# Second norm and first relational half: one core, a cut at column 96 of the third layer, scatters moved beside it

## The reference, cut to what matters

```python
h = relu(layernorm(x)); x = x + L0(h, src, dst)
h = relu(layernorm(x)); x = x + L1(h, src, dst, theta)
h = relu(layernorm(x)); x = x + L2(h, ..., src, dst, edge_type_86)
h = relu(layernorm(x)); x = x + L3(h, src, dst)
# L2, for every edge e:
#   msg  = sum_b w_comp[etype, b] * (h[src] @ weight[b])
#   gate = tanh(relu(<h[src] @ A1 + b1, h[dst] @ A2 + b2 + rel[etype]> / sqrt(32)))
#   out  = relu(segment_sum(gate * msg, dst) + h[src of the last edge] @ self_loop_weight)
```

## Time and profile before

| | us |
|---|---|
| median of 3 runs | 2469.23 |
| lowest, highest | 2468.75, 2469.87 |
| the profiled execution's own time | 2470.35 |
| its span in the trace | 2468.6 |

### The profile page before, as it was taken

One profiled execution on the slowest core, in us unless ns is written; L12 is line 12 of the kernel. 1 busy time (PEld: TensorE's weight loads), 2 busy tenths in 40 slices (PEclk: granted clock), 3 DMA queues, 4 the chain that ended last, 5 costly groups with the idle time before them and its releaser, 6 DMA issues.

```text
span 2468.6 us, 12924 instructions
## 1 busy us (share of the span) xinstructions
PE 327.9 (13%) x2316; PEld 243.5 (10%) x2316; DVE 1818.3 (74%) x3200; ACT 388.7 (16%) x1275; POOL 1419.5 (58%) x1426
## 2 busy tenths in 40 slices
PE   0000000201100000010000001066764000034000
PEld 0000000101000000000000001044442000034000
DVE  8998989988699995971889989999999952321000
ACT  0000001010022121200112200177774210000000
POOL 6666776371776047306777720366662177777776
PEclk9999999999999999999999999976666555555555
DMA  1001003000221125100122220000000120100000
GB/s 21 17 9 29 12 16 119 6 12 2 96 66 32 51 67 178 42 34 10 63 71 62 84 77 0 3 8 8 8 8 4 59 69 10 35 12 11 8 8 8
DMA packets 57643, 88.37 MB, mean 36 GB/s; under 512 B 26387, under 2 KB 49864, under 8 KB 56184
## 3 DMA queue, kind: packets, MB, share of 16 engines
q0 software_dynamic: 44864, 19.00, 5.1%
q1 hardware_dynamic: 6872, 43.31, 4.5%
q10 hardware_dynamic: 5856, 25.60, 2.7%
HBM read 37.41 MB, written 54.76 MB: 37 GB/s over the span
## 4 chain that ended last, share of the span: by engine, by line
DVE 59%; POOL 15%; issue 12%; PE 6%; DMA 3%; ACT 2%; DVEq 0%; ACTq 0%; SPq 0%; POOLq 0%
POOL out L1789 9%; DVE mf L589 9%; POOL mf L1783 6%; DVE pay L589 4%; DVE psum L1321 4%; DVE pay L1307 4%; DVE psum L1306 3%; DVE outs L589 3%; DVE z L589 2%; PE psum L2271 2%; DVE z L1602 2%; DVE psum L618 2%; PE psum L2234 1%; DVE mf L1311 1%; DVE xs L1311 1%
## 5 line engine op out<-in xcount | busy, mean ns | idle before, releaser
L1789 POOL DMA_INDIRECT out<-outs,i_src x196 | 200.3, 1022 | 236.9 <-DVE outs L1578 109.2
L1783 POOL DMA_INDIRECT xd<-in_x,i_dst x196 | 205.2, 1047 | 109.7 <-DVE mf L589 55.5
L1783 POOL DMA_INDIRECT xs<-in_x,i_outS x196 | 195.9, 999 | 68.9 <-issue 56.4
L1789 POOL DMA_INDIRECT out<-outs,i_srcX x196 | 199.3, 1017 | 62.3 <-issue 57.6
L589 DVE TENSOR_TENSOR mf<-mf 128x128 f32<-128x128 f32 (+6 forms) x582 | 181.0, 348 | 10.5
L2005 ACT ACTIVATE pay<-pay 128x1248 f32<-128x1248 f32 (+1 forms) x63 | 75.6, 1199 | 647.4 <-DVE pay L1307 627.2
L589 DVE TENSOR_TENSOR pay<-psum,pay 128x512 f32<-128x512 f32 x196 | 130.4, 684 | 16.8 <-ACT pay L2095 14.7
L1602 DVE TENSOR_REDUCE z<-pay 128x512 f32 (+1 forms) x196 | 132.3, 675 | 0.0
L2234 PE MATMUL psum<-pay 128*128 128x512 f16 x196 | 102.7, 524 | 89.3 <-ACT pay L2080 55.6
L1783 POOL DMA_INDIRECT mf<-l_own_rows,lists x50 | 49.8, 996 | 111.9 <-DMA l_own_rows<-xs 97.0
L1783 POOL DMA_INDIRECT mf<-l_own_rows,ptr x46 | 45.9, 998 | 99.1 <-DMA l_own_rows<-pay 85.4
(11 more groups left out here) (521 smaller groups left out, 2726.2 us busy)
## 6 DMA issues: line engine op xcount, KB each, us to landing
outs<-in_x ACTq DMA_DIRECT2D x14, 624.0 KB, 5.4
out<-outs ACTq DMA_DIRECT2D x14, 624.0 KB, 3.0
l_first_rows<-mf SPq DMA_DIRECT2D x2, 3234.0 KB, 9.8
z<-in_x ACTq DMA_DIRECT2D x6, 624.0 KB, 6.0
out<-z ACTq DMA_DIRECT2D x6, 624.0 KB, 2.9
l_own_rows<-pay SPq DMA_DIRECT2D x1, 3430.0 KB, 9.5
payload_by_dst<-z SPq DMA_DIRECT2D x1, 3234.0 KB, 9.5
sums_by_edge<-z SPq DMA_DIRECT2D x1, 3234.0 KB, 17.3
```

The source lines that it names most:

```text
L1783: G.indirect_dma_start(out=dest(k), out_offset=None, in_=table, in_offset=bass.IndirectOffsetOnAxis(ap=idx[:, k:k + 1], axis=0), bounds_ch ...
L1789: G.indirect_dma_start(out=table, out_offset=bass.IndirectOffsetOnAxis(ap=idx[:, k:k + 1], axis=0), in_=source(k), in_offset=None, bounds_ ...
```

## The change

Three parts. (1) The packing into MULTI and FOLLOWING moves from before the dense halves to behind the last part of `first_layer`; one copy is added, which keeps the places (`place_m`), and the memset of `kept` moves behind it. (2) The relational loop is cut behind turn 24 (column 96). Columns 0 to 95 (part A) get their gate, sums, self loop, own rows, norm, fills and first rows at the cut; columns 96 to 195 (B; BH with column 95) get theirs behind the loop. The rows of a partition's first node, whose carry isn't known at the cut, are picked out with masks (`ends`) and written later by two scatters of their own (`heads_out`) and one fill (`head_fill`). (3) POOL sends 38 columns of OUT ahead instead of 12, then one for each tile to the cut, 40 at the pace of DVE's steps in the cut, 22 behind it, then A's 96 fills, one for each tile; 19 of these wait for the last tile.

```diff
-SENDS_AHEAD = 12
+SENDS_AHEAD = 38
+CUT_TURN = 24
+CUT = 4 * CUT_TURN
+HEADC = CUT - 1
+SENDS_BETWEEN = 40
+OWN_BEFORE_HEAD = 36
...
+            for k, (own, part) in enumerate(((XSW, A), (OWNT, B))):
+                sp.wait_ge(s["l3_own_ready"], k + 1)
+                sp.dma_start(own_rows[:, part, :], own[:, part, :]).then_inc(s["l3_own_stored"], 16)
+                sp.wait_ge(s["l3_first_ready"], k + 1)
+                span = slice(part.start * ROWW, part.stop * ROWW)
+                sp.dma_start(first_rows[:, span], first_f[:, span]).then_inc(s["l3_first_stored"], 16)
...
+            ends, free = c["tmp"][:, A], c["tmp2"][:, 0:EC]
+            link(ts(free, col("kn"), FAR / 2, FAR, ALU.is_lt, ALU.mult))
+            link(tt(free, free, col("dst_out"), ALU.add))
+            link(V.tensor_copy(icols["outF"][:, B], free[:, B]))
...
+            for given, out_index in ((free[:, A], head_fill), (c["linear"][:, A], head_row)):
+                link(tt(picked, ends, given, ALU.mult))
+                link(V.tensor_reduce(found_at, picked, AX.X, ALU.add))
+                link(tt(out_index, found_at, none, ALU.add))
+            for k, name in enumerate(("dis", "kn", "dst_out")):
+                link(tt(picked, ends, c[name][:, A], ALU.mult))
+                link(V.tensor_reduce(head_own[:, D + k:D + k + 1], picked, AX.X, ALU.add))
...
+            l2_turns(0, CUT_TURN)
...
+            marks["cut"] = link.n
+            gated(MA, A, 1)
+            running_sums(MA, A)
+            link(V.tensor_copy(cut_sum, Z[:, HEADC, :]))
+            link(tt(Z[:, A, :], Z[:, A, :], CUR[:, A, :], ALU.add))
+            ends = c["tmp"][:, A]
+            link(tt(ends, c["head"][:, A], c["head"][:, 1:CUT + 1], ALU.subtract))
+            for given, out_row in ((Z, head_sum), (XD, head_own[:, 0:D])):
+                link(tt(MA, given[:, A, :], bc(ends), ALU.mult))
+                link(V.tensor_reduce(out_row, MA.rearrange("p c f -> p f c"), AX.X, ALU.add))
+            link(V.scalar_tensor_tensor(out=XD[:, A, :], in0=Z[:, A, :], scalar=0.0, in1=XD[:, A, :], op0=ALU.max, op1=ALU.add))
+            link(V.tensor_copy(cut_row, XD[:, HEADC, :]))
+            link(V.tensor_copy(XSW[:, A, 0:D], XD[:, A, :]))
+            own_rows(XSW, A)
+            V.memset(small[:, 2:3], 0.0).then_inc(s["l3_own_ready"], 1)
+            layernorm(XD[:, A, :], HA, MA, w=WA)
+            V.scalar_tensor_tensor(out=Z[:, A, :], in0=HA, scalar=ALPHA, in1=XD[:, A, :],
+                                   op0=ALU.mult, op1=ALU.add).then_inc(s["d_rows_ready"], 1)
+            link(V.tensor_copy(MEAN[:, A], c["dis"][:, A]))
+            link(V.tensor_copy(FIRST[:, A, D], c["kn"][:, A]))
+            tt(FIRST[:, A, 0:D], HA, bc(MEAN[:, A]), ALU.mult).then_inc(s["l3_first_ready"], 1)
+            marks["cut_done"] = link.n
+
+            l2_turns(CUT_TURN, EC // 4)
...
+                if k >= CUT + SENDS_AHEAD + SENDS_BETWEEN:
+                    pool.wait_ge(s["l2_done"], 3 + k - SENDS_AHEAD - SENDS_BETWEEN)
+                elif k >= CUT + SENDS_AHEAD:
+                    pool.wait_ge(s["dve"], marks["cut"] + (k - CUT - SENDS_AHEAD) * (marks["cut_done"] - marks["cut"]) // SENDS_BETWEEN)
+                elif k >= SENDS_AHEAD:
                     pool.wait_ge(s["l2_done"], 2 + k - SENDS_AHEAD)
                 scatter(out, lambda q: OUT[:, q, :], icols["sent"], last[N], s["outs_scattered"], 1, k)
+            pool.wait_ge(s["d_rows_ready"], 1)
+            for k in range(CUT):
+                behind = EC - CUT - SENDS_AHEAD - SENDS_BETWEEN + k
+                pool.wait_ge(s["l2_done"], 2 + min(CUT + behind + 1, EC))
+                scatter(out, lambda q: Z[:, q, :], icols["outF"], last[N], s["dfull_out"], 1, k)
             pool.wait_ge(s["l3_zero"], 1)
+            pool.wait_ge(s["l3_own_ready"], 2)
+            scatter(tables["l3", "own"], lambda q: OWNT[:, HEADC, :], head_row, last[P * EC], s["heads_out"], 1)
+            pool.wait_ge(s["l3_own_stored"], 32)
+            pool.wait_ge(s["heads_out"], 16)
+            gather(lambda k: OWN1[:, k, :], tables["l3", "own"], own3l, last[P * EC], s["l3_own_in"], OWN_BEFORE_HEAD)
...
```

More of the change, by code:

```diff
@@ L59, with feeds_of @@
 FEEDS = tuple((k, min(k + FEED, EC)) for k in range(0, EC, FEED))
+def feeds_of(first, last):
+    return tuple((k, min(k + FEED, last)) for k in range(first, last, FEED))
 UNROLL = 4
@@ L287, in build @@
         v_at += W3 * ROWW
+        head_own, head_sum = chosen[:, 0:OWNW], chosen[:, OWNW:OWNW + D]
+        cut_sum, cut_row = extra[:, 2 * W1:2 * W1 + D], extra[:, 2 * W1 + D:2 * W1 + 2 * D]
+        head_fill, head_row = edge0[:, 0:1], edge0[:, 1:2]
+        WA, WB = CUT, EC - HEADC
+        A, B, BH = slice(0, CUT), slice(CUT, EC), slice(HEADC, EC)
+        MA, HA = rows(mf[:, 0:WA * D]), rows(mf[:, WA * ROWW:WA * ROWW + WA * D])
+        HB = rows(z_t[:, CUT * D:CUT * D + WB * D])
+        assert WA * (ROWW + D) <= (CUT + 4) * 2 * D and CUT * D + WB * D <= EC * PAYLOAD
         V3, V3T = (rows(z_t[:, v_at + k * W3 * D:v_at + (k + 1) * W3 * D]) for k in range(2))
@@ L1629, in l2_turns, with gated, running_sums @@
                     l2_turn(last - 1, 0, False)
-            l2_turns(0, EC // 4)
+            def gated(out, part, number):
+                ts(c["score"][:, part], c["score"][:, part], float(D) ** -0.5, 0.0, ALU.mult, ALU.max).then_inc(s["tail_ready"], 1)
+                dve.wait_ge(s["gate_made"], number)
+                link(tt(out, Z[:, part, :], bc(MEAN[:, part]), ALU.mult))
+            def running_sums(m, part):
+                link.many([V.tensor_tensor_scan(Z[:, part, f], c["cont"][:, part], m[:, :, f], 0.0, ALU.mult, ALU.add) for f in range(D)])
@@ new lines, in own_rows @@
+            def own_rows(own, part):
+                link(V.tensor_copy(own[:, part, D], c["dis"][:, part]))
+                link(V.tensor_copy(own[:, part, D + 2], c["dst_out"][:, part]))
+                link(V.tensor_copy(own[:, part, D + 1], c["kn"][:, part]))
+            l2_turns(0, CUT_TURN)
+            dve.wait_ge(s["l2_scored"], CUT_TURN + 1)
+            dve.wait_ge(s["l2_done"], CUT + 2)
+            dve.wait_ge(s["l2_xy"], CUT_TURN + 1)
+            marks["cut"] = link.n
+            gated(MA, A, 1)
@@ L1638, in _ @@
+            dve.wait_ge(s["carry_out"], 1)
+            for lo, hi in SUM_CUT[1:]:
+                lo = max(lo, CUT)
+                added = rows(ADDED[:, 0:(hi - lo) * D])
+                link(tt(added, bf(CAR, hi - lo), bc(c["head"][:, lo:hi]), ALU.mult))
+                link(tt(Z[:, lo:hi, :], Z[:, lo:hi, :], added, ALU.add))
             V.memset(small[:, 2:3], 0.0).then_inc(s["tail_ready"], 1)
+            dve.wait_ge(s["l3_own_stored"], 16)
+            link(tt(head_sum, head_sum, CAR, ALU.add))
@@ L1913, in fills @@
                 scatter(out, lambda q: OUT[:, q, :], icols["outF"], last[N], s["dfull_out"], n, first)
-            pool.wait_ge(s["d_rows_ready"], 1)
-            fills(0, FILLS_LISTING)
+            pool.wait_ge(s["d_rows_ready"], 2)
+            scatter(out, lambda q: OUT[:, HEADC, :], head_fill, last[N], s["dfull_out"], 1)
+            fills(CUT, FILLS_LISTING)
             pool.wait_ge(s["l3_second_stored"], 16)
@@ L1976, in norm, with feed @@
                 norms[0] += 1
-            def feed(source):
+            def feed(source, parts=FEEDS):
                 act.wait_ge(s["normed"], norms[0])
-                for k, (lo, hi) in enumerate(FEEDS):
+                for k, (lo, hi) in enumerate(parts):
                     if feeds[0] > 1:
@@ L2102, in l2_turns @@
                     l2_turn(last - 1, 0, 2)
-            l2_turns(0, EC // 4)
+            l2_turns(0, CUT_TURN)
             act.wait_ge(s["tail_ready"], 1)
-            S.activation(MEAN, col("score"), ACT.Tanh).then_inc(s["gate_made"], 1)
+            S.activation(MEAN[:, A], c["score"][:, A], ACT.Tanh).then_inc(s["gate_made"], 1)
+            norm(MA, HA, WA)
+            l2_turns(CUT_TURN, EC // 4)
+            act.wait_ge(s["tail_ready"], 2)
+            S.activation(MEAN[:, B], c["score"][:, B], ACT.Tanh).then_inc(s["gate_made"], 1)
             act.wait_ge(s["l2_cs"], EC)
-            act.wait_ge(s["tail_ready"], 2)
-            feed(XS)
-            norm(XS, Z)
-            feed(Z)
+            act.wait_ge(s["tail_ready"], 3)
+            feed(XS, feeds_of(CUT, EC))
+            norm(XS[:, BH, :], HB, WB)
+            feed(HB, feeds_of(0, WB))
             norm(Tc[:, 0:W, :], Fc[:, 0:W, :], W)
```

120 lines of the change are left out of this document (73 added, 47 removed).

## The result

The changed kernel takes 2401.04 us (median of 4 runs, 2400.59 to 2401.63); the kernel before, beside it on the same chip, 2469.55. The ratio is 0.9721 (95% interval 0.9709 to 0.9733): 68.5 us faster. 84.5 were forecast, so 2386. The direction, the mechanism and the range hold; the size is 15 us short. The profiled execution has a span of 2399.1 us against 2468.6 before, 69.5 less, and the missing 15 us are looked for in these two spans.

A forecast was written before the change was run, and what follows sets the result against it. DVE's work up to layer 3's first own-row gather, then POOL's count of DMAs, was taken as the bound. +36.5 us before that gather and -121.0 after it gave -84.5: 2470.35 to 2386 us, range 2374 to 2405.

The forecast's parts named there:

- Packing moved: Packing block put behind layer 0's sums: gain 0, since nothing waits for POOL there; bounds -3.5 to +1 us.
- list of fills and masks: 19 small operations added ahead of the second norm, on DVE's path: +5.1 us.
- cut, part A: DVE's work on 96 columns between the loop's halves, nine passes, scans, norm, copies: +58.0 us, reductions taken at the low end.
- tail, part B: DVE's work behind the loop, for 100 of 196 columns: 32.2 us instead of 57.1, so -24.9.
- own rows to first gather: Store of half the table beside memset and head scatter: 7.1 us instead of 10.3, so -3.2.
- code and steps not seen: Two DVE issue gaps for new straight code: +1.5 us.
- first gather: POOL's first gather of layer 3's own rows: 36.5 us later, at 1998 +- 4 us, with 285 DMAs behind it.
- POOL's tail: POOL's DMAs from the first gather on: 94 fewer at 1.287 us each, -121.0 us, with no wait replacing the fills.
- the rival in which it loses it: Cut loop's tiles lengthen; decides at 0.43 us a tile, 2484 us at 0.5; both slower rivals together 0.03.
- Sends and fills beside the loop: POOL's scatters beside DVE's loop cost nothing, covered by DVE, with 2 us to spare behind the last tile.
- POOL being late: Rival: POOL falls behind in the cut, so the first gather waits for A's fills; 2402, likelier 2394 us; chance 0.17.
- POOL's sends in the cut: Passes that hold POOL fill 27 of 58 us, so 26 of 40 sends get out; the 14 left are caught up later.

The follow-up runs named there:

- pack_alone: The kernel before with only the packing block and the memset of kept moved to their new place: ratio 1.0025 to the kernel before.
- pack_back: The changed kernel with the packing block and the memset of kept back at their old places: 2395.89 us, ratio 0.9697 to the kernel before.
- load_held: The changed kernel with SP's load of the sums waiting until ACT's store of the first half has landed: 2394.82 us, ratio 0.9692 to the kernel before.
- ahead_12: The changed kernel with 12 sends ahead instead of 38: 2421.31 us, ratio 0.9799 to the kernel before.
- no_early_fills: The changed kernel without part A's 96 fills and DVE's wait for them, rows left unwritten: ratio 0.9723 to the kernel before.
- before_less_fills: The kernel before without 96 of its last 98 fills, rows left unwritten: ratio 0.9515 to the kernel before.
- before_less_48: The kernel before without 48 of its last 98 fills, rows left unwritten: 2412.65 us beside 2472.01 of the kernel before, one run each.

## Why the prediction was right in direction and 15 us too low

84.5 us were forecast and 69.5 measured between the two profiled executions. The step that failed is "Packing moved", costed at nothing and measured at +5.1 us; the reductions, the second own copy and the program's end, which was in no term, make up most of the rest. By its own steps, from the two traces:

| step | forecast | measured |
|---|---|---|
| packing moved | 0 | +5.1 |
| list of fills and masks | +5.1 | +5.3 |
| cut, part A | +58.0 | +61.7 |
| tail, part B | -24.9 (32.2 us) | -22.6 (34.5 us) |
| own rows to first gather | -3.2 | -2.4 |
| code and steps not seen | +1.5 | +0.8 (both halves of the loop together) |
| first gather | +36.5 | +47.9 |
| POOL's tail | -121.0 | -117.4 |
| sum | -84.5 | -69.5 |

- **Packing moved** failed, and outside its own bounds (-3.5 to +1). I followed the block, POOL's gathers and DVE's path behind it, but not what it was moved *past*: three dense halves that now start 41.9 us earlier, while POOL's scatters of the sums, and with them SP's load, stay where they were. A store met that load (8.0 us of DVE's time against 2.9 us won). pack_alone, pack_back and load_held show it. "POOL's first gather moves some 3.5 us up" was wrong with it: it starts at 888.98, where it was 887.60. That nothing waits for POOL there held: DVE takes the rows up at 1052.60 with no idle time ahead.
- **Cut, part A** was right in its nine passes, scans (8.14) and norm. Mis-sized was the one term that I named as unknown: a reduction across the features costs 5.27 us, 1.72 ns an element, between my bounds of 1.07 and 2.35; I took the low end for both of them, +3.7 us. My own sign of being wrong, "reductions over features of 5 us and more", came true. The row nearest to it in kind, the scans, should have had more weight.
- **Tail, part B**: 1.7 of its 2.3 us are the copy of 101 rows, which took 3.52 us where the copy of 96 took 1.76. I scaled a row at 196 columns by count.
- **The loop keeps its pace**, and the rival in which it loses it is dead. The ends of turns on DVE, as in the earlier trace rows, around the cut and at the loop's end:

```profile
1748.76 0.50 DVE L615 TENSOR_TENSOR pay<-iota_p,et 128x344 f16<-128x344 f32 x1
1754.83 0.50 DVE L615 TENSOR_TENSOR pay<-iota_p,et 128x344 f16<-128x344 f32 x1
1822.63 0.50 DVE L615 TENSOR_TENSOR pay<-iota_p,et 128x344 f16<-128x344 f32 x1
1828.93 0.51 DVE L615 TENSOR_TENSOR pay<-iota_p,et 128x344 f16<-128x344 f32 x1
...
1954.48 0.51 DVE L615 TENSOR_TENSOR pay<-iota_p,et 128x344 f16<-128x344 f32 x1
1960.26 0.51 DVE L615 TENSOR_TENSOR pay<-iota_p,et 128x344 f16<-128x344 f32 x1
```

The turns take 5.8 to 6.1 us on both sides, but for the first behind the cut with 6.3.

- **POOL's tail**: the count holds to 0.5 us up to the last scatter (375.7 us from the first gather, 497.15 before); the 4.0 us at the program's end were in no row that I read.
- **Sends and fills beside the loop** cost nothing, as forecast, but for another reason than mine. My slack of 2 us was wrong behind the loop, not in the cut. Long before the loop's end POOL was waiting for tiles again (in nearly every turn from 1879 us on), so what it had lost in the cut no longer counted. Behind the last tile, which ends at 1966.13, I had 19 fills take 35 us, 8.5 of them for scans and 1.8 for a copy that hold POOL, and the memset let it go on at 37. The fills ended at 1991.04, 24.9 us behind the tile, since nothing held them, and the memset at 2006.14, 40.0 us behind it. That makes the slack 15.4 us, and the chance of 17% for POOL being late was too high for this cut. ahead_12 shows where it starts.
- **POOL's sends in the cut**: five scatters were held, by 13.4 us together, not the 27 us of the passes that I had added up: a pass of 3.4 us can hold one scatter for at most what is left of it, and POOL's own 0.98 us fit between. Another 6.8 us went in two waits for the pace that the kernel itself sets, 5.91 us of idle time beside the 32 scans the larger (1761.67 to 1767.58). 32 scatters started in the cut, where I had 26. My 26 was itself a wrong sum: 31 us at 1.287 make 24, and the 16 left over, 20.6 us, would not quite have been caught up in my 20.
- The fills were where the gain is, as the prediction has it: no_early_fills and before_less_fills show both sides of it.
- Of the signs that I named, the first gather missed its window (2009.37 against 1998 +- 4), and layer 1's gathers and L1422 moved later by 1.4 and 5.0 us, where I had them earlier and unmoved. The cut takes 61.7 us where 58 were named, under the 70 at which the prediction fails. The 285 DMAs, the turns (to 0.1 us) and A's fills came out as named. That 2401 lies in the range has some luck in it: 5.1 us of the packing and 4.0 of the program's end lay outside the bounds, and they fitted into room that was kept for POOL being late, which it wasn't. (The upper end adds up to 2406, not 2405.)

## What to carry to other kernels

When a block is moved, list what it is moved past: everything behind its old place starts earlier, and each plain transfer there has to be laid beside those of the other queues, whose times are set by another engine and don't move along. Count an off-path engine's slack from the last point at which it waits for the engine on the path, since what it lost ahead of that is gone; then test it by taking some of its lead away. Cut a copy so that it keeps its speed: 101 columns from an odd one on took 3.52 us, 100 from an even one on 1.83, and the copy of all 196 took 3.43.

## What the chip did that I had not expected

- A store of 624 KB landed in a median of 7.4 us beside a 3234 KB load issued 0.6 us behind it, in 3.0 us with the load held for 6.3 us; the load itself took 13.7 and 12.4 us.
- 32 scans with both operands in SBUF held a scatter for up to 7.0 us in some groups and for none in others; of two groups with the same operands, one held it for 4.35 us and the other not. The Trainium skill, "SBUF — State Buffer", section "Who interferes with whom", calls the ports that the two engines share an exclusive lock and says that the order of issue decides who blocks. For the products of the cut the trace agrees: the scatter issued 1.3 us into a pass of 3.42 us ends behind it, though one issued 0.02 us behind its start isn't held. A hold that lasts over many scans is more than one instruction, and is not covered by it.
- The end of the program behind the last scatter is 10.0 us with 98 fills in front of the last scatters, and 14.0 with 50 (before_less_48) or 2 (before_less_fills).
